# A fused alignment, recurrence and expert kernel: the first table rows fetched early, a second distance memory, and VectorE's distance operations spread

## What is computed

```python
def _align_one(small, large):
    D = _pairwise_euclidean(small, large)   # sqrt(max(aa + bb - 2ab, 0)), 64 x 1601
    R = _dtw_cost(D)                        # R[i,j] = D[i,j] + min(R[i-1,j], R[i,j-1], R[i-1,j-1])
    i_idx, j_idx, valid = _backtrack(R, T_small, T_large)
    ...
x = x + _L0_xattn_ref(ctx_1024, _layernorm(x, axis=-1))   # _align_one over 32 batches
x = x + _L0_attn_ref(_layernorm(x, axis=-1), ...)         # a recurrence over each sequence
x = x + _L0_ffn_ref(_layernorm(x, axis=-1), ...)          # 2 of 8 experts, and a shared one
```

## Time and profile before

| what | value |
|---|---|
| median of 3 runs | 1146.53 us (1144.05 to 1146.61) |
| profiled execution | 1146.06 us, of which the span from the first to the last instruction is 1144.5 us |
| busy, share of the span | PE 998.4 us (87%), DVE 657.8 (57%), ACT 497.9 (44%), POOL 115.7 (10%) |
| first distances | 14 to 123 us |
| from the first group to the second | 123 to 149 us |
| second distances beside the alignment's forward rows | 149 to 268 us |
| second distances beside its way back, then its rest | 268 to 353 us |
| second alignment, recurrence, experts | 353 to 1144.5 us |

### The profile page before, as it was taken

How to read it: one execution, slowest core, us unless ns; L and a number is a source line. 1 busy time by engine, 2 the same in 40 slices (tenths; PEclk the granted TensorE clock), 3 DMA queues, 4 the chain that set the end, 5 groups by cost and what they waited for, 6 DMA issues and landing times.

```text
span 1144.5 us, 15538 instructions
## 1 busy us (share of the span) xinstructions
PE 998.4 (87%) x4892; PEld 593.9 (52%) x4892; DVE 657.8 (57%) x2310; ACT 497.9 (44%) x850; POOL 115.7 (10%) x150
## 2 busy tenths in 40 slices
PE   5889498889953999867988798887999999999998
PEld 2334133333312555534766465555676767676776
DVE  7998689998999675795779213447111111111116
ACT  5889467667741445233321363432222222222221
POOL 2000000000000000000000000000443434342110
PEclk9999799999986999989989799898999999999999
DMA  9998884555859896240230492782222222223014
GB/s 353 318 332 272 284 278 137 175 157 177 252 159 322 269 322 206 93 140 0 69 123 1 142 360 99 212 330 102 83 66 78 64 75 65 68 72 109 27 63 177
DMA packets 123454, 189.75 MB, mean 166 GB/s; under 512 B 8800, under 2 KB 92928, under 8 KB 123376
## 3 DMA queue, kind: packets, MB, share of 16 engines
q1 hardware_dynamic: 117488, 170.41, 46.0%
q0 software_dynamic: 5888, 18.36, 5.2%
HBM read 165.43 MB, written 23.30 MB: 165 GB/s over the span
## 4 chain that ended last, share of the span: by engine, by line
PE 57%; DVE 32%; issue 4%; ACT 4%; DMA 3%; SPq 1%; POOL 0%; DVEq 0%; ACTq 0%; POOLq 0%
PE bank L1833 13%; PE bank L1680 8%; PE bank L1864 7%; PE bank L1701 5%; DVE table L841 4%; DVE beyond L857 4%; PE bank L1825 4%; DVE passed L862 3%; PE bank L1844 3%; DVE z L771 2%; DVE dist L780 2%; PE bank L1607 2%; DVE col_min L834 2%; PE bank L1856 2%; DVE z L763 2%
## 5 line engine op out<-in xcount | busy, mean ns | idle before, releaser
L1035 DVE TENSOR_TENSOR hid<-bank,act_s 128x352 f32<-128x352 f32 x104 | 54.2, 523 | 221.0 <-PE bank L1833 182.2
L1833 PE MATMUL bank<-w_up,srcT 128*128 x512 | 162.9, 461 | 0.8 <-ACT srcT L1446 0.8
L1454 ACT ACTIVATE act_s<-bank 128x352 f32<-128x352 f32 x104 | 48.0, 463 | 198.7 <-PE bank L1833 127.7
L1833 PEld LDWEIGHTS bank<-w_up,srcT 128*128 128x128 f32 x512 | 96.2, 190 | 47.7 <-issue 4.1
L1585 PE MATMUL bank<-ctxT,latT 128*64 128x402 f32 (+1 forms) x512 | 102.9, 524 | 19.0 <-DMA ctxT<-ctx_tr_dram 18.2
L1591 PE MATMUL bank<-sq,ones 128*64 128x402 f32 (+1 forms) x512 | 101.2, 517 | 17.8 <-ACT sq L1303 17.8
L1303 ACT ACTIVATE sq<-ctxT 128x1608 f32<-128x1608 f32 x64 | 97.5, 1527 | 21.5 <-DMA ctxT<-ctx_tr_dram 21.5
L1607 PE MATMUL bank<-table,ident 128*128 128x402 f32 x144 | 66.4, 545 | 40.7 <-DVE stays L804 34.2
L1680 PE MATMUL bank<-rows_c,on_path 128*64 128x256 f32 (+1 forms) x832 | 99.2, 391 | 1.1 <-ACT on_path L1365 0.5
L1864 PE MATMUL bank<-w_dn,hidT 128*128 (+1 forms) x384 | 93.6, 380 | 0.4 <-DVE y_sb L1049 0.4
L841 DVE TENSOR_TENSOR_SCAN table<-col_min,table 128x201 f32<-128x201 f32 x140 | 88.6, 633 | 2.7
(11 more groups left out here) (296 smaller groups left out, 1584.4 us busy)
## 6 DMA issues: line engine op xcount, KB each, us to landing
rows_c<-ctx_nat_dram SPq DMA_DIRECT2D x32, 896.0 KB
ctxT<-ctx_tr_dram SPq DMA_DIRECT2D x32, 804.0 KB, 7.4
ctxT<-ctx_tr_dram SPq DMA_DIRECT2D x32, 797.0 KB, 7.4
rows_c<-ctx_nat_dram SPq DMA_DIRECT2D x32, 640.0 KB
spaced<-dist SPq DMA_DIRECT2D x128, 101.0 KB, 3.7
w_up<-w_t_dram SPq DMA_DIRECT2D x16, 704.0 KB, 13.3
table<-spaced SPq DMA_DIRECT2D x40, 202.0 KB, 3.6
table<-spaced SPq DMA_DIRECT2D x6, 808.0 KB, 12.4
```

What stands on the lines that cost most here:

```text
L1833: last = e.matmul(psum[2 * i + m][:, 0:HH], srcT[t % 2][:, k, :], w_up[:, bass.ds(ex, 1), m, k, columns], start=(k == 0), stop=(k == KC - 1))
```

## The change

1. The second group gets a DRAM tensor of its own (`spaced` is a list of two), so SP no longer waits for the first group's table loads before it stores unit 32. The pads are stored twice, 0.7 MB each.
2. The first chunk of 8 rows is cut into two of 4. The first four rows of all 128 lanes are fetched by one DMA that ACT issues, once the units up to 29 are stored (`stored(e, u - 2)` with u = 31). All other rows of table 0 are loaded by SP after unit 31 is stored; the loads of quarters of lanes on the way are gone for the first group.
3. ACT squares the context of units 32 and 33 ahead of that DMA. SP's two held-back context loads go in their usual places, at units 25 and 27; the one for units 36 and 37 goes between the table's chunks.
4. The first group has three buffers of z and of root (in the last rows of table 0), and DVE's five operations of a unit no longer stand together: bias(u), left(u-1), slope(u-1), add(u-2), correct(u-1).
5. In the second group DVE's three operations of a unit stand one by one between alignment rows.

```diff
-ROW_CHUNKS = -(-STEPS // FEW_ROWS)
-EARLY_CHUNKS = 2
-MADE_ROW = 4 + EARLY_CHUNKS * FEW_ROWS
+CHUNK_ROWS = [0, 4] + list(range(FEW_ROWS, STEPS, FEW_ROWS)) + [STEPS]
+ROW_CHUNKS = len(CHUNK_ROWS) - 1
+MADE_ROW = 8
+LATE_ROW = 56
...
-        spaced = nc.dram_tensor("spaced", (P, LANE), F32).ap()
+        spaced = [nc.dram_tensor(f"spaced{g}", (P, LANE), F32).ap() for g in range(GROUPS)]
...
+        def z_of(u):
+            return first_z[u % 3] if u < GUNITS else z[u % 2]
...
+        def stored(e, u):
+
+            for m in range(u - DISTS + 1, u + 1):
+                e.wait_ge(dist_out[m % DISTS], dist_slot_value(m))
...
-                if u >= 2:
-                    e.wait_ge(dist_done, u - 1)
+                if u >= 3:
+                    e.wait_ge(dist_done, u - 2)
...
+            def first_distances():
+                for u in range(GUNITS + 1):
+                    if u < GUNITS:
+                        distance_bias(u)
+                    else:
+                        distance_add(u - 2)
+                    if u:
+                        distance_left(u - 1)
+                        distance_slope(u - 1)
+                    if 2 <= u < GUNITS:
+                        distance_add(u - 2)
+                    if u:
+                        distance_correct(u - 1)
+                    yield
+                distance_add(GUNITS - 1)
+
+            def second_distances():
+                for _ in range(4):
+                    yield
+                for u in range(GUNITS, UNITS):
+                    if u < LATE_UNIT:
+                        distance_left(u)
                         yield
+                    elif u == LATE_UNIT:
                         yield
+                        yield
+                    distance_correct(u)
+                    yield
+                    distance_add(u)
+                    yield
+                    yield
+                    if u >= LATE_UNIT:
+                        yield
...
-            interleave(distances(1), align(0), lambda n: CB // 2)
+            interleave(second_distances(), align(0), lambda n: 1)
...
                     distance_roots(u)
+                    if u == GUNITS - 1:
+                        squares(u + 1)
+                        squares(u + 2)
+                        e.wait_ge(cleared, 1)
+                        e.wait_ge(padded, PADDED)
+                        stored(e, u - 2)
+                        load_lanes(e, 0)
...
-                if u == GUNITS:
-
-                    for c in range(ROW_CHUNKS):
-                        e.wait_ge(table_in[c], table_in_value(0, c))
...
+                if u == GUNITS - 1:
+                    store_distance(u)
+                    stored(e, u)
+                    e.wait_ge(terms_kept, 16)
+                    for c in range(1, ROW_CHUNKS):
+                        load_lanes(e, c)
+                        if c == 4:
+                            load_next(GUNITS // 2)
```

More of the change, by code:

```diff
@@ L408, in build @@
         made_sq = place("made_sq", [CT * P])
+        assert cursor[0] <= table_at[0] + LATE_ROW * W * 4
+        at(table_at[0] + LATE_ROW * W * 4)
+        first_z = [place(f"first_z{i}", [QC]) for i in range(3)]
+        first_root = [place(f"first_root{i}", [QC]) for i in range(3)]
         assert cursor[0] <= table_at[0] + TABLE
@@ L1262, in vector_program @@
             row_features()
-            interleave(distances(0), chain(latents(1), latents(2), latents(3)), lambda n: 1)
-            interleave(distances(1), align(0), lambda n: CB // 2)
+            interleave(first_distances(), chain(latents(1), latents(2), latents(3)), lambda n: 1)
+            interleave(second_distances(), align(0), lambda n: 1)
             interleave(align(1), chain(add_rows(range(0, 4)), pause(), together(recurrence(0), add_rows(range(4, 8))),
@@ L1324, in distances @@
             def distances(g):
-                squares(g * GUNITS)
+                if g == 0:
+                    squares(0)
                 for u in range(g * GUNITS, (g + 1) * GUNITS):
-                    if u + 1 < (g + 1) * GUNITS:
+                    if u + 1 < (g + 1) * GUNITS and u != GUNITS:
                         squares(u + 1)
@@ L2129, in sync_program @@
             for u in range(UNITS):
-                if u % 2:
-                    for m in following(u // 2) if u // 2 not in AFTER else []:
-                        e.wait_ge(ctx_read, u + 1)
-                        e.wait_ge(squared, u + 1)
-                        load_ctxT(m)
+                if u % 2 and u != GUNITS + 1:
+                    load_next(u // 2)
                 if u == QUARTERS:
```

81 lines of the change are left out of this document (35 added, 46 removed).

## The result

The changed kernel takes 1133.20 us (median of 4 runs, 1132.44 to 1137.40) against 1146.57 us (4 runs, 1144.05 to 1148.60): ratio 0.989, 95% interval 0.986 to 0.992. Timed again beside more runs of before it came to 0.987 (0.984 to 0.990). It is faster, as forecast, and inside the range of 1122 to 1137.5, but by 13 to 15 us where 18.6 were forecast.

A forecast was written before the change was run, and what follows sets the result against it. PE was taken to bound the first group, DVE the second's forward rows, with a PE and ACT loop close behind. Terms -4.1 -2.7 -6.9 -4.8 +1.7 -2.5 +0.7 gave -18.6 us on 1146.06: 1127.5, median 1128, range 1122 to 1137.5.

The forecast's parts named there:

- A: First group's distances, up to PE's last product there: spread DVE operations shorten the units with latents, -4.1 us (0 to -8.2).
- B: From the first group's last PE product to row 0's minimum: first rows fetched by ACT arrive sooner, -2.7 us (0 to -4.1).
- Loaded after 2.81: Step before row 0: its minimum comes 2.81 us after the start of the first rows' load, as before the change.
- C1: Row 0 to row 8 of the first alignment, 19.18 us before: waits go as unit 32 has its own memory, -6.9 us.
- C2: 15 forward cycles of four rows and a unit: 7.34 us falls to 7.02, the PE and ACT loop, -4.8 us.
- D: Way back of the first alignment, 13 units: spaced distance operations cost less than pairs, -2.5 us (0 to -3.1).
- C3: Row 68 to the way back: PE's last gap, hidden behind DVE until now, stands out, +1.7 us.
- The first rival: Spacing DVE operations buys nothing, by the skill's rule: -8.3 us, so 1138 us; chance 0.10.
- E: After the way back: the last store's travel to the second table does not shrink, +0.7 us (0 to 2.5).
- the opened loop: Rival for the forward cycles: ACT and PE stay ahead, DVE runs at 6.80 us a cycle, 1124 us; chance 0.13.
- new waits: Rival: ACT-issued rows land no sooner, DMA holds the first group, or rows 4 to 7 come late: 1131 to 1135; 0.11.
- Slower: Rival on the way back: the round of store, load, square, product, sum outgrows DVE's time, 1147 us or more; chance 0.03.

## Why the prediction was right in its sign and 5 us off in its size

**A, -4.1 forecast, -3.3 in the mean: the order does it, by other waits than those that the size was taken from.** T was 117.74 and 118.00 in two profiles of before, 117.84 with the old order in the changed kernel, and 114.96, 115.00, 115.83, 113.20, 113.46, 115.32, 114.40 and 114.52 in the eight profiles whose first group is that of the changed kernel. The prediction took half of its bounds because this is near the 3.9 us that PE waits for the latents. But those waits hardly fell in the first profile, from 3.9 to 3.5 us; it is PE's six waits for ACT's squares, 5.9 us before, that fell to 3.6. Together they fell by 2.7 us, which is A's 2.8.

**B, -2.7 forecast, -1.3 in the mean of the same profiles** (T to row 0: 10.39, 11.27, 10.63, 10.64, 9.55, 9.84, 10.80 and 11.75, against 12.07 and 11.67). The step that failed is "Loaded after 2.81". That time was read from a load of 202 KB, a quarter of the lanes. ACT's load of all lanes, 4 rows each, has 404 KB and took 4.4 us to land, and in all eight profiles 4.4 to 5.2 us, once 6.5, passed from its issue to row 0. So "the 2.81 us halve with the bytes" had the bytes the wrong way round: they doubled. The two steps ahead of it held. The sum of unit 29 ended at T + 2.25, forecast T + 2.3, and "Stored after 4.27" was a little long: ACT's DMA went out 3.2 to 4.2 us behind that sum. The context load of units 34 and 35, which the prediction counted nowhere in B, makes the stores slower and brings DVE's waits for a buffer, but those fall on the sums of units 28 and 30. Held back, it gave T + 8.9 in one profile, 0.7 us less than the shortest of the eight.

**C1, -6.9: right in size, by a reason that is in part wrong.** Row 8 came 11.30, 12.27, 11.80, 12.21 and 11.30 us behind row 0 in the five profiles whose code there is that of the changed kernel, against 19.18 and 17.54: -6.6. The context load in its place is needed for it (holding it back put 6 us in). The memory of its own, which the prediction names first, is not: with one memory it was 12.2. What the second memory did was to keep 5.6 us out of C2 and D, a price that the prediction has nowhere. That the squares of units 32 and 33 stand ahead was not taken out by itself.

**C2, C3, D: right to 0.4 us each in the first profile**, and by their mechanisms: the spaced operation at +0.36, the cycle held at 7.02 by PE and ACT, shown by opening that loop. The first rival, from the Trainium skill ("VectorE: DVE Perf Modes", section "The DRAIN you can't avoid"), falls here: the two groupings of the same operations differ by 0.32 us a cycle, and the run with them together is 5 us slower. The same section adds that a next operation which is not held starts earlier; here an independent one started 0.49 us behind one of 0.58 us (114.36 to 114.85).

**E, +0.7 forecast with 2.5 as its bound, +5.3 measured in the first profile: the largest miss.** The steps that failed are "the last store's travel to the second table doesn't shrink with it" and "All from 353 us on is untouched". The instructions behind 353 us are the same, but what stands ahead of them is not. Two things were missed. First, the last unit of the way back now stands closer to its end: its sum fell from 335.84 to 320.08, 15.8 us, while row 0 of the second alignment fell by 18.6. SP can only then store, load the table in ten chunks instead of nine, and load x, terms and context rows:

```profile
330.55 0.59 SPq L2204 DMA_DIRECT2D xr<-x_dram  x1
331.24 4.03 SPq L2208 DMA_DIRECT2D first_terms<-kept_terms  x1
335.31 6.43 SPq L2092 DMA_DIRECT2D rows_c<-ctx_nat_dram  x3
```

The rows are issued 0.1 us before row 0, and in the other profiles with the new way back from 1.1 us before it to 0.6 us after it; in the two profiles of before it was 3.5 and 4.2 us before, and 4.1 where the old way back was put back. Wherever the clock had risen in time (six profiles with the new way back, that with 175 idle products left out), PE waits 1.2 to 2.6 us for them; in both profiles of before it does not. Second, the granted clock: the first context product took 3.24 us in both profiles of before and in these six, and 4.91 to 4.93 in the other five, 1.7 us more. The first addition to x in the kernel before, and in the first profile of the changed one:

```profile
376.00 0.42 DVE L940 TENSOR_TENSOR xr<-xr,bank 128x256 f32<-128x256 f32 x1 [4.89 <-PE bank L1680]
...
359.83 0.42 DVE L987 TENSOR_TENSOR xr<-xr,bank 128x256 f32<-128x256 f32 x1 [7.21 <-PE bank L1735]
```

This is 22.0 us behind row 0 before, and 24.4 in the changed kernel. Over all, the part behind row 0 took 790.5 and 791.5 us before, and 793.4 to 799.3 in eight profiles of kernels whose code there is that of the changed one (mean 795.8). Of these 4.8 us, 2.4 lie ahead of the first addition to x, which came 22.0 and 21.5 us behind row 0 before, and 22.9 to 25.4 in the eight. Each of the eight has either the wait for the rows or the slow product there, and neither profile of before has one. The other half lies further on, where PE works at 1.2 GHz at another place than before: between 681 and 741 us of the first profile one product group took 6.64 us for 5.21, another 3.01 for 1.88, 2.6 us together. Whether the change makes such draws likelier is open: two profiles of before are too few, and the idle products that were to keep the clock up were either too long or not long enough. The share of the late rows is open too. It was argued from the waits, and the run that was to move them did not; and with the second group's operations together the rows were issued 4.1 us ahead, PE did not wait for them, and the part behind row 0 took 796.6 us all the same, with the product at 4.93.

The chances: spacing nothing (0.10) and the opened loop (0.13) did not come, new waits (0.11) did in part, in B and E. Slower (0.03) has a trace: contexts late on the way back cost DVE 1.35 to 2.56 us in four profiles (second group together, squares ahead, one memory, 175 idle products), and nothing in the two of the changed kernel itself. In the account of the first profile A, B and E came 6.9 us short of the forecast and the other terms 1.6 us better, which makes the 5.3: that the part up to the second alignment came within 0.7 us (18.6 for 19.3) is in part luck, misses of both signs. The sums themselves hold, but for C3 and E, each rounded up by 0.1.

## What to carry to other kernels

Operations of one engine that need each other's result, and stand together, are worth spreading where that engine is the bound; ask at once which loop of the other engines comes next, since it took 0.26 of the 0.59 us a cycle here until one square was moved. A transfer's travel time read from a row holds only for its size and for what shared the queues in that row: look up how many KB the new transfer has before you reuse the time. When a stage shrinks, look at what is queued behind its last item and not only at its length, since loads for the next stage start from that item.

## What was not expected of the hardware

- DVE's spaced operations started 0.47 to 0.49 us apart at 0.55 to 0.58 us duration, and dependent ones 0.61 to 0.68: 0.1 to 0.2 us an operation for a change of order alone.
- PE was at the lower clock behind 3.84 us of idle time, though it had worked 22.5 us without a gap ahead of that (gap product 1.71 us; 0.84 with no idle time).
- With 2 MB of x issued ahead of the last store, of 0.2 MB, the loads that wait for it started 6.0 us behind the end of its issue, and not 1.8.
- Equal code took 790.5 to 799.3 us in a stretch that the change does not touch, in part by the place where PE worked at the lower clock. Differences under 0.5% of this kernel are therefore better read from landmarks than from totals.
